# The layout of an intermediate in HBM: 512-byte pieces or 4-KB pieces

## The chip, the cores and the metric

One Trainium2 chip, all 8 cores. Each core computes one of the 8 batch elements with the same program, and the cores don't exchange data. The time is the device time of the slowest core in microseconds (us). The profile and the trace are of one execution, on the slowest core (core 4).

## The reference

```python
xn = layernorm(x)                                   # x: 8 x 2048 x 1024, f32
# attention, one head of width 1024, causal, softmax over all of (t, s)
q, k, v = xn @ Wq + bq, xn @ Wk + bk, xn @ Wv + bv
attn = softmax_all(mask(q @ k.T / 32)) @ v
# feed-forward on xn, int weights with scales per group of 128 rows
h  = layernorm(xn) * gamma + beta
y  = silu(h @ dequant(fc1_q, fc1_scales) + b1)      # 2048 x 4096 per core
z  = y @ dequant(fc2_q, fc2_scales) + b2            # 2048 x 1024 per core
out = x + attn + (xn + 0.5 * z)
```

Matrix products are done in bf16 with each operand split into a high and a low part; three of the four partial products are summed (`PAIRS`), so one product of a 128-row block over 1024 inputs is 24 matmuls (`mm24`).

## The kernel before

The stages follow each other: layernorm and q, k, v projections, attention, then fc1 and fc2. The engines run programs written out by hand and meet at semaphores.

fc1 goes over four blocks `tc` of 512 tokens and in each over 32 blocks `fc` of 128 hidden columns; one (`tc`, `fc`) is a unit `k` (`emit_fc1_unit`). A unit: TensorE does 24 matmuls of 512 columns into `P[k % 2]` (it waits for the Silu of unit k-2, which frees the bank); ScalarE applies Silu into `B_yf` (waits for TensorE and for GpSimd's unit k-2); GpSimd splits `B_yf` into a high and a low bf16 part in four buffers `B_yst[s2b][half]` (`s2b`: which 256 of the 512 tokens). Each buffer holds 8 units, 128 partitions by 8 x 256 bf16. After every eighth unit ScalarE's queue waits for GpSimd and then issues four stores of 512 KB, one for each buffer, into `hy` in HBM; GpSimd may begin the ninth unit only when all four have landed (`sy4`).

In `tc` 0 the fc1 weights are made at the same time (`emit_dq1_unit`, `emit_dq1_sub`): blocks of 8 dequantisation units, then 4 fc1 units. A dequantisation unit: VectorE forms (q - 128) * scale in PSUM from `B_dqq` and `B_dqs`, ScalarE copies it to bf16 `A_w1h` and then issues, from its own queue, the loads of `B_dqq` and `B_dqs` for the unit three further on; VectorE forms the low part `C_w1l`. So the ACT queue carries Silu, copies, weight loads and the stores of `hy` in one order.

fc2 reads `y` back in 8 groups of 256 tokens (`ygrp_load`), each in four quarters of 8 `fc`, high and low part: 64 loads of 512 KB from `hy` into `B_ygh` and `B_ygl`, issued on SP. The first group's `B_ygh` is loaded when `tc` 2 of fc1 has ended, its `B_ygl` when all of fc1's matmuls have. For the groups after it each quarter is loaded as soon as the matmuls of the group before have read it (`mmq`). Before the weights of fc2 are loaded into `B_dq2q` and `B_dq2s`, whose memory overlaps `B_yst`, SP waits for all stores of `hy` (L1285). The first group of fc2 runs beside the dequantisation of its weights, the other seven without it.

`hy` is `[4, 2, 2, NF, 128, 256]` in bf16: tc, s2b, half, fc, partition, token. In one store or load of 8 `fc`, a partition's 256 tokens of one `fc`, 512 B, are contiguous in HBM, and the next `fc` of that partition lies 64 KB further. In SBUF the same data are 4 KB in one piece per partition.

Of the kernel before, what the change touches and what calls it, by code (L numbers as in the profile page):

```python
# [8 lines left out]
BF16 = mybir.dt.bfloat16  # L9
# [10 lines left out]
NF = 32  # L20
# [16 lines left out]
def build_nc():  # L37
    nc = bass.Bass("TRN2", target_bir_lowering=False)
# [22 lines left out]
    hh = [nc.dram_tensor(f"hh{i}", [T, D], BF16, kind="Internal").ap() for i in range(2)]  # L61
    hqT = nc.dram_tensor("hqT", [NT, 2, 128, D], BF16, kind="Internal").ap()
    hattn = nc.dram_tensor("hattn", [NT, 128, D], F32, kind="Internal").ap()
    hy = nc.dram_tensor("hy", [4, 2, 2, NF, 128, 256], BF16, kind="Internal").ap()

    _rsv = nc.alloc_sbuf_tensor("arena_reserve", [128, 208704], mybir.dt.uint8)
    BASE = None
# [130 lines left out]
    def rd(eng, sem, out, in_, **kw):  # L198
        eng.dma_start(out=out, in_=in_, **kw).then_inc(sem.h, 16)  # L199
        sem.n += 16  # L200
        return sem.n

    def wr(eng, sem, out, in_):
        eng.dma_start(out=out, in_=in_).then_inc(sem.h, 16)  # L204
        sem.n += 16
        return sem.n

    with nc.Block() as block:
# [136 lines left out]
        def mm24(tensor, psum_ap, lhsT, rhsT, lslc, rslc):  # L345
            n = 0
            for g in range(ND):
                for (a, b) in PAIRS:
                    i = tensor.matmul(psum_ap, lhsT[a][lslc(g)], rhsT[b][rslc(g)],  # L349
                                      start=(n == 0), stop=(n == 23))  # L350
                    n += 1
            return i
# [771 lines left out]
        def emit_fc1_unit(tc, fc):  # L1124
            k = tc * NF + fc

            @block.tensor
            def _(tensor, tc=tc, fc=fc, k=k):
                if fc == 0:
                    tensor.wait_ge(lh[tc % 2].h, ht_ld[tc])  # L1130
                if tc == 0:
                    tensor.wait_ge(ve.h, ve_dqblk[fc // 4])
                if k >= 2:
                    tensor.wait_ge(ac.h, ac_y[k - 2])
                slot = tc % 2
                i = mm24(tensor, P[k % 2][:, 0:512], (A_w1h, C_w1l),
                         (B_hth[slot], B_htl[slot]),
                         lambda g, fc=fc: (slice(None), slice(g * FF + fc * 128, g * FF + (fc + 1) * 128)),
                         lambda g: (slice(None), slice(g * 512, (g + 1) * 512)))
                mm.inc(i)  # L1140
                mm_y[k] = mm.n

            @block.scalar
            def _(scalar, fc=fc, k=k):
                scalar.wait_ge(mm.h, mm_y[k])
                if k >= 2:
                    scalar.wait_ge(gp.h, ve_y[k - 2])
                i = scalar.activation(B_yf[k % 2][:], P[k % 2][:, 0:512], AF.Silu,  # L1148
                                      bias=M_b1T[:, fc:fc + 1])
                ac.inc(i)  # L1150
                ac_y[k] = ac.n

            @block.gpsimd
            def _(gpsimd, tc=tc, fc=fc, k=k):
                gpsimd.wait_ge(ac.h, ac_y[k])
                if k == 0:
                    gpsimd.wait_ge(sa[0].h, sa_t[NT - 1][0])
                    gpsimd.wait_ge(sa[1].h, sa_t[NT - 1][1])
                if fc % 8 == 0 and k >= 8:
                    tp, vp = sy_t[k - 1]  # L1160
                    gpsimd.wait_ge(sy4[tp].h, vp)
                c0 = (fc % 8) * 256
                gpsimd.tensor_copy(B_yst[0][0][:, c0:c0 + 256], B_yf[k % 2][:, 0:256])
                i = gpsimd.tensor_copy(B_yst[1][0][:, c0:c0 + 256], B_yf[k % 2][:, 256:512])  # L1164
                v_ = gp.inc(i)
                gpsimd.wait_ge(gp.h, v_)
                for s2b in range(2):
                    i = gpsimd.tensor_tensor(B_yst[s2b][1][:, c0:c0 + 256],  # L1168
                                             B_yf[k % 2][:, s2b * 256:(s2b + 1) * 256],
                                             B_yst[s2b][0][:, c0:c0 + 256], ALU.subtract)  # L1170
                gp.inc(i)
                ve_y[k] = gp.n

            if fc % 8 == 7:
                @block.scalar
                def _(scalar, tc=tc, fc=fc, k=k):
                    scalar.wait_ge(gp.h, ve_y[k])
                    fg = fc // 8
                    for s2b in range(2):
                        for half in range(2):  # L1180
                            wr(scalar, sy4[tc],
                               hy[tc, s2b, half, fg * 8:(fg + 1) * 8].rearrange("f p u -> p f u"),
                               B_yst[s2b][half].rearrange("p (f u) -> p f u", f=8))
                    sy_t[k] = (tc, sy4[tc].n)

# [53 lines left out]
        def ygrp_load(sync, grp, chase=False):  # L1239
            tc_, sub_ = grp // 2, grp % 2  # L1240
            sync.wait_ge(sy4[tc_].h, 256)
            for q4 in range(4):
                if chase:
                    if q4 < 3:
                        sync.wait_ge(mmq.h, (grp - 1) * 3 + q4 + 1)
                    else:
                        sync.wait_ge(mm.h, mm_z[grp - 1])
                for half in range(2):
                    dstb = (B_ygh, B_ygl)[half]
                    rd(sync, lyq[q4],  # L1250
                       dstb.rearrange("p (f u) -> p f u", f=NF)[:, q4 * 8:(q4 + 1) * 8, :],
                       hy[tc_, sub_, half, q4 * 8:(q4 + 1) * 8].rearrange("f p u -> p f u"))
                yq_ld[(grp, q4)] = lyq[q4].n

        @block.sync
        def _(sync):
            sync.wait_ge(mm.h, mm_tc_end[2])
            sync.wait_ge(sy4[0].h, 256)
            for q4 in range(4):
                rd(sync, lyq[q4],  # L1260
                   B_ygh.rearrange("p (f u) -> p f u", f=NF)[:, q4 * 8:(q4 + 1) * 8, :],
                   hy[0, 0, 0, q4 * 8:(q4 + 1) * 8].rearrange("f p u -> p f u"))

        @block.sync
        def _(sync):
            sync.wait_ge(mm.h, mm_tc_end[3])
            sync.wait_ge(sa[0].h, sa_t[NT - 1][0])
            sync.wait_ge(sa[1].h, sa_t[NT - 1][1])
            for q4 in range(4):
                rd(sync, lyq[q4],  # L1270
                   B_ygl.rearrange("p (f u) -> p f u", f=NF)[:, q4 * 8:(q4 + 1) * 8, :],
                   hy[0, 0, 1, q4 * 8:(q4 + 1) * 8].rearrange("f p u -> p f u"))
                yq_ld[(0, q4)] = lyq[q4].n


# [45 lines left out]
        for grp in range(8):  # L1321
            tc, sub = grp // 2, grp % 2

            @block.sync
            def _(sync, grp=grp, tc=tc, sub=sub):
                if grp >= 1:
                    ygrp_load(sync, grp, chase=True)
# [145 lines left out]
```

## Time and profile before

| | us |
|---|---|
| two runs | 2893.95, 3166.56 |
| their median | 3030.25 |
| the profiled execution | 2899.33 |
| its span, first to last instruction, core 4 | 2897.7 |
| spans of the 8 cores | 2875.2 to 2897.7 |
| TensorE busy | 2333.2 (81%) |
| ScalarE busy | 753.8 (26%) |
| VectorE busy | 681.9 (24%) |
| GpSimd busy | 274.7 (9%) |
| `hy` stores, ACT queue | 64 of 512 KB, 6.3 us to landing (median) |
| `B_ygh`, `B_ygl` loads, SP queue | 32 and 32 of 512 KB, 4.1 and 5.3 us |

The profiled execution stands beside the faster of the two runs, and everything read from the trace is compared with its own time. A busy share is an average over stages that have different limits, so the stages are read one by one.

### The profile page before, as it was taken

The page shows a single profiled execution, that of the slowest core. Times are in us where ns is not written, and L with a number is a line of the kernel's source. Part 1 is how long each engine was busy: PE and PEld are TensorE (multiplying, and loading weights), DVE is VectorE, ACT ScalarE, POOL GpSimd, SP SyncE. Part 2 cuts the span into 40 slices and gives each one's busy share as a digit, 9 for nine tenths or more (in the row PEclk, how much of TensorE's full clock was granted, in tenths as well). Part 3 has the DMA queues.
Part 4 walks back from the last instruction along what each step waited for, and adds up shares of the span by engine and source line. Part 5 has one row for each costly group of instructions (what it writes and reads, how often), then busy time and mean ns, then how long its engine had stood idle before and what let it go on. Part 6 is the DMA issues. An engine that isn't in the chain of part 4 may idle for free.

```text
span 2897.7 us, 26924 instructions; the slowest of 8 cores (2875.2 to 2897.7 us)
## 1 busy us (share of the span) xinstructions
PE 2333.2 (81%) x10500; PEld 1040.4 (36%) x10500; DVE 681.9 (24%) x910; ACT 753.8 (26%) x882; POOL 274.7 (9%) x547
## 2 busy tenths in 40 slices
PE   0349999997888887535659999999554899999998
PEld 0124444443333343212224444444211344444443
DVE  3422421113433324332220000000044311221122
ACT  3221321112222232146663333333244000000000
POOL 1000000000000000002213334334200000000000
PEclk9879999998778898757879999999855999999999
DMA  7524632213212110175442222231455422223330
GB/s 232 156 73 80 137 85 44 53 30 105 84 58 59 51 44 23 50 189 145 145 124 59 58 61 56 59 88 30 139 200 201 131 77 87 87 87 95 102 102 15
DMA packets 364558, 268.25 MB, mean 93 GB/s; under 512 B 181216, under 2 KB 312304, under 8 KB 364048
## 3 DMA queue, kind: packets, MB, share of 16 engines
q1 hardware_dynamic: 230016, 136.89, 17.3%
q10 hardware_dynamic: 131232, 107.50, 12.6%
q0 software_dynamic: 3184, 22.14, 2.3%
q8 instruction: 84, 1.38, 0.2%
q14 instruction: 42, 0.34, 0.0%
HBM read 157.41 MB, written 75.50 MB: 80 GB/s over the span
## 4 chain that ended last, share of the span: by engine, by line
PE 69%; ACT 9%; DMA 7%; DVE 6%; ACTq 4%; issue 3%; POOL 1%; SPq 1%; DVEq 0%; POOLq 0%
PE P L349 39%; PE P L1359 22%; PE P L860 8%; ACTq L204 3%; DMA B_dq2s<-s 2%; DMA B_dqs<-s 2%; DMA hxn<-B_sl 2%; ACT L1148 1%; ACT L1104 1%; SPq L199 1%; ACT L1307 1%; ACT B_yf L1148 1%; ACT L803 1%; DVE B_dq2f L1298 1%; DVE C_w2l L1315 1%
## 5 line engine op out<-in xcount | busy, mean ns | idle before, releaser
L349 PE MATMUL P<-B_hth,A_w1h 128*128 128x512 bf16 x1024 | 396.5, 387 | 152.8 <-ACT B_yf L1148 106.0
L1359 PE MATMUL P<-A_w2h,B_ygh 128*128 128x512 bf16 x1024 | 400.8, 391 | 113.7 <-DVE C_w2l L1315 113.7
L1359 PE MATMUL P<-A_w2h,B_ygl 128*128 128x512 bf16 x1024 | 402.8, 393 | 0.0
L1359 PE MATMUL P<-C_w2l,B_ygh 128*128 128x512 bf16 x1024 | 402.2, 393 | 0.0
L349 PE MATMUL P<-B_htl,A_w1h 128*128 128x512 bf16 x1024 | 396.2, 387 | 0.0
L349 PE MATMUL P<-B_hth,C_w1l 128*128 128x512 bf16 x1024 | 395.6, 386 | 0.0
L349 PE MATMUL P<-B_xth,C_wh 128*128 128x512 bf16 x512 | 196.4, 384 | 164.0 <-DMA B_xtl<-hxn 96.5
L1148 ACT ACT_TABLE_LOAD x128 | 164.2, 1283 | 398.5 <-PE P L349 306.3
L349 PEld LDWEIGHTS P<-B_hth,A_w1h 128*128 128x128 bf16 x1024 | 101.8, 99 | 285.3 <-issue 170.8
L349 PE MATMUL P<-B_xtl,C_wh 128*128 128x512 bf16 x512 | 196.2, 383 | 0.0
L349 PE MATMUL P<-B_xth,C_wl 128*128 128x512 bf16 x512 | 196.1, 383 | 0.0
L1359 PEld LDWEIGHTS P<-A_w2h,B_ygh 128*128 128x128 bf16 x1024 | 101.8, 99 | 261.8 <-issue 148.2
L1298 DVE SCALAR_TENSOR_TENSOR B_dq2f<-B_dq2q,B_dq2s 128x1024 f32<-128x1024 int32 x32 | 39.1, 1223 | 581.0 <-DMA B_dq2s<-s 580.6
L1168 POOL TENSOR_TENSOR B_yst<-B_yf,B_yst 128x256 bf16<-128x256 f32 x256 | 165.8, 669 | 19.3 <-POOL B_yst L1164 0.9
L1359 PEld LDWEIGHTS P<-A_w2h,B_ygl 128*128 128x128 bf16 x1024 | 103.0, 101 | 129.5 <-issue 15.2
L349 PEld LDWEIGHTS P<-B_hth,C_w1l 128*128 128x128 bf16 x1024 | 101.9, 100 | 126.2 <-issue 9.6
L349 PEld LDWEIGHTS P<-B_htl,A_w1h 128*128 128x128 bf16 x1024 | 101.7, 99 | 123.3 <-issue 8.2
L1359 PEld LDWEIGHTS P<-C_w2l,B_ygh 128*128 128x128 bf16 x1024 | 101.8, 99 | 121.7 <-issue 8.1
L1383 DVE TENSOR_SCALAR B_t<-B_xt,M_mu,M_r 128x512 f32<-128x512 f32 x32 | 17.4, 543 | 492.8 <-PE P L1359 484.3
L349 PEld LDWEIGHTS P<-B_xth,C_wh 128*128 128x128 bf16 x512 | 50.5, 99 | 226.6 <-issue 167.7
L776 ACT ACT_TABLE_LOAD x40 | 51.3, 1283 | 308.7 <-DVE B_ast L876 307.4
L860 PE MATMUL P<-C_vh,B_pth 128*128 128x512 bf16 x272 | 119.8, 441 | 13.0 <-DVE B_ptl L843 13.0
(147 smaller groups left out, 2599.3 us busy)
## 6 DMA issues: line engine op xcount, KB each, us to landing
hy<-B_yst ACTq DMA_DIRECT2D x64, 512.0 KB, 6.3
B_ygh<-hy SPq DMA_DIRECT2D x32, 512.0 KB, 4.1
B_ygl<-hy SPq DMA_DIRECT2D x32, 512.0 KB, 5.3
B_dq2q<-q SPq DMA_DIRECT2D x32, 512.0 KB, 3.9
B_dq2s<-s SPq DMA_DIRECT2D x32, 512.0 KB, 4.7
B_dqq<-q ACTq DMA_DIRECT2D x61, 256.0 KB, 3.8
B_dqs<-s ACTq DMA_DIRECT2D x61, 256.0 KB, 4.5
A_x<-x POOLq DMA_DIRECT2D x16, 512.0 KB, 27.6
```

Source lines behind the costliest of these rows:

```text
L199: eng.dma_start(out=out, in_=in_, **kw).then_inc(sem.h, 16)
L204: eng.dma_start(out=out, in_=in_).then_inc(sem.h, 16)
L349: i = tensor.matmul(psum_ap, lhsT[a][lslc(g)], rhsT[b][rslc(g)], start=(n == 0), stop=(n == 23))
L776: i = scalar.activation(B_pf[ch % 2][:, 0:w], B_sc[:, ch * 512:ch * 512 + w], AF.Exp, bias=M_negm[:, t:t + 1], accum_out=M_zc[:, ch:ch + 1])
L803: i = scalar.activation(B_sc[:, ch * 512:ch * 512 + w], P[ch % 2][:, 0:w], AF.Copy, scale=1.0 / 32.0)
L860: i = tensor.matmul(P[2 + h2][:, 0:512], (B_pth, B_ptl)[a][:, b * 128:(b + 1) * 128], (C_vh, C_vl)[c][:, b * D + h2 * 512:b * D + (h2 + 1) ...
L1104: i = scalar.activation(A_w1h[:, dst], PD1[k % 3][:, 0:512], AF.Copy)
L1148: i = scalar.activation(B_yf[k % 2][:], P[k % 2][:, 0:512], AF.Silu, bias=M_b1T[:, fc:fc + 1])
L1168: i = gpsimd.tensor_tensor(B_yst[s2b][1][:, c0:c0 + 256], B_yf[k % 2][:, s2b * 256:(s2b + 1) * 256], B_yst[s2b][0][:, c0:c0 + 256], ALU.su ...
L1298: i = vector.scalar_tensor_tensor(B_dq2f[fc % 2][:], B_dq2q[fc % 2][:], -128.0, B_dq2s[fc % 2][:], ALU.add, ALU.mult)
L1307: i = scalar.activation(A_w2h[:, dst], B_dq2f[fc % 2][:], AF.Copy)
L1359: i = tensor.matmul(P[pb + h2][:, 0:512], (B_ygh, B_ygl)[a][:, fc * 256 + jj * 128:fc * 256 + (jj + 1) * 128], (A_w2h, C_w2l)[c][:, fc * D ...
```

## The change

The dimension of partitions and that of `fc` change places in `hy`. Each partition's 32 x 256 values of one (tc, s2b, half) now lie in 16 KB in one row, and a store or load of 8 `fc` takes 4 KB of it per partition. Order, waits, queues and sizes of all transfers stay as they are.

```diff
-    hy = nc.dram_tensor("hy", [4, 2, 2, NF, 128, 256], BF16, kind="Internal").ap()
+    hy = nc.dram_tensor("hy", [4, 2, 2, 128, NF, 256], BF16, kind="Internal").ap()
...
                             wr(scalar, sy4[tc],
-                               hy[tc, s2b, half, fg * 8:(fg + 1) * 8].rearrange("f p u -> p f u"),
+                               hy[tc, s2b, half, :, fg * 8:(fg + 1) * 8],
                                B_yst[s2b][half].rearrange("p (f u) -> p f u", f=8))
...
                     rd(sync, lyq[q4],
                        dstb.rearrange("p (f u) -> p f u", f=NF)[:, q4 * 8:(q4 + 1) * 8, :],
-                       hy[tc_, sub_, half, q4 * 8:(q4 + 1) * 8].rearrange("f p u -> p f u"))
+                       hy[tc_, sub_, half, :, q4 * 8:(q4 + 1) * 8])
...
-                   hy[0, 0, 0, q4 * 8:(q4 + 1) * 8].rearrange("f p u -> p f u"))
+                   hy[0, 0, 0, :, q4 * 8:(q4 + 1) * 8])
...
-                   hy[0, 0, 1, q4 * 8:(q4 + 1) * 8].rearrange("f p u -> p f u"))
+                   hy[0, 0, 1, :, q4 * 8:(q4 + 1) * 8])
```

## Rows read from the trace of the kernel before

**Rows 1.** Page: granted TensorE clock in 40 slices, in tenths; DMA packets by size.
```profile
PEclk9879999998778898757879999999855999999999
DMA packets 364558, 268.25 MB, mean 93 GB/s; under 512 B 181216, under 2 KB 312304, under 8 KB 364048
```

**Rows 2.** Stages: us, busy (x) of PE, PEld, DVE, ACT, POOL; PEclk, DMA share, GB/s.
```profile
1243.00:1520.00 277.00, 151.45 (x624) 64.35 (x624) 84.06 (x128) 169.31 (x178) 48.48 (x96) 0.76 0.57 153
1520.00:2072.00 552.00, 534.95 (x2448) 239.65 (x2448) 0.00 (x0) 203.18 (x207) 210.80 (x416) 0.99 0.23 60
2259.00:2898.00 639.00, 625.13 (x2886) 282.77 (x2886) 127.63 (x193) 0.00 (x0) 0.00 (x0) 0.99 0.27 86
```

**Rows 3.** Chain of waits in fc1, tc 1 to 3: start us, us, what.
```profile
1566.66 31.25 PE P L349 x144
...
1857.24 0.37 ACTq L204
...
1859.68 1.48 ACTq L204
1861.30 1.28 ACT L1148
...
1863.43 31.25 PE P L349 x144
...
2035.64 31.25 PE P L349 x144
```

**Rows 4.** Waits, 1520 to 2072 us: who for whom, us, times, longest.
```profile
POOL B_yst L1163 <- DMA hy<-B_yst: 117.8, 12, 12.8
...
PE P L349 <- ACT B_yf L1148: 31.9, 13, 20.3
```

**Rows 5.** DMA issues: ns min/median/max; the page's landing, us; SP's timeline.
```profile
L204 ACTq DMA_DIRECT2D hy<-B_yst x64: 366/1336/4127, 1344.7 to 2077.6; - x64
...
L204 ACTq DMA_DIRECT2D hattn<-B_ast x16: 332/333/338, 688.1 to 1215.3; - x16
...
hattn<-B_ast ACTq DMA_DIRECT2D x16, 512.0 KB, 2.7
...
2396.20 0.34 SPq L199 DMA_DIRECT2D B_xt<-x  x1
...
2397.58 1.01 SPq L199 DMA_DIRECT2D B_at<-hattn  x1
```

**Rows 6.** Chain of waits in tc 0; last row: the page's median landing, us.
```profile
1344.75 0.39 ACTq L204
...
1351.94 5.45 DMA B_dqs<-s
...
1420.11 0.38 ACTq L204
...
1427.26 5.08 DMA B_dqs<-s
...
1494.21 0.38 ACTq L204
...
1501.68 6.06 DMA B_dqs<-s
...
B_dqs<-s ACTq DMA_DIRECT2D x61, 256.0 KB, 4.5
```

**Rows 7.** End of fc1: SP's loads in the timeline, then the chain of waits.
```profile
2067.07 3.94 SPq L199 DMA_DIRECT2D B_ygl<-hy  x4
...
2071.67 0.37 ACTq L204
...
2077.57 6.55 DMA hy<-B_yst
```

**Rows 8.** Stretches of 2 us, columns as in rows 2: the last two are DMA.
```profile
1649.00:1651.00 2.00, 1.86 (x9) 0.65 (x7) 0.00 (x0) 1.47 (x2) 0.00 (x0) 1.00 1.10 302
...
2317.00:2319.00 2.00, 2.00 (x11) 0.94 (x10) 0.00 (x0) 0.00 (x0) 0.00 (x0) 1.00 1.02 418
```

## The prediction

> **What bounds the kernel now.** I read the page's slices first, then the busy time by stage, then the chain of waits inside each stage, and last the issue and landing times of the DMAs that the change touches. The granted clock is the top digit wherever TensorE is busy, and the packet line says that most packets are small [rows 1]. By stage [rows 2]: in the first quarter of fc1 (`tc` 0, 277 us) TensorE works 151 us, so the dequantisation on ScalarE, VectorE and the ACT DMA queue sets the pace; in the rest of fc1 (552 us) TensorE is busy 535 us and is the bound but for small gaps; in the last 639 us, fc2 after its first group, it is busy 625 us and has nothing to gain. The small gaps of fc1 come once every 8 units (one unit is 24 matmuls for one `fc`): the chain leaves TensorE for the four stores of `hy` on ScalarE's queue, then a Silu, then TensorE again [rows 3]. TensorE waited for that Silu 13 times in this stage, 31.9 us, of which one wait of 20.3 us belongs to the dequantisation before it and 11.6 us to the 12 stores; GpSimd waited 12 times for the stores to land [rows 4].
>
> **What the change does to the transfers.** All of `hy` goes through 64 stores and 64 loads of 512 KB. `hy` now has pieces of 256 bf16, 512 B, so each transfer has 1024 pieces; 128 x 1024 = 131,072 packets, and the page counts 312304 - 181216 = 131,088 between 512 B and 2 KB [rows 1]. So practically all packets of that size are `hy`. After the change the 8 `fc` of one partition lie side by side: 128 pieces of 4 KB, 16,384 packets, at a pitch of 16 KB in HBM. Nothing else is added, removed or moved; no wait and no queue changes. The bytes are the same. What can change is (a) how long ScalarE's queue is held while it issues the four stores and (b) how fast 2.1 MB drain.
>
> (a) *Issue.* The first store of a group takes 0.37 us and the last 1.48 us even where the group is quick; the median of 64 is 1.34 us, the longest 4.13 us [rows 3, 5]. So it isn't the instruction that costs, it is the room behind it: the later ones are pushed back. The nearest rows with 4 KB pieces: the 16 writes of `hattn`, 0.33 us each, one at a time; and four 512 KB loads in a row on SP, the first 0.34 and the last 1.01 us, together 2.4 us from first start to last end [rows 5]. So four stores will cost 1.4 us (0.33 each with small gaps) to 2.4 us, against 3.9 us now at the least (1857.24 to 1861.16, [rows 3]). I take 2.4, since four in a row are what we have.
>
> (b) *Drain.* With `hy` stores alone in flight the core moves 302 GB/s; with 4 KB pieces in both directions (output writes beside loads of x and `hattn`) 418 GB/s [rows 8]. The DMA engines are fully busy in both, so the difference is the piece. I take 418 GB/s; the lower end is that the rate stays at about 300.
>
> The Trainium skill ("DMA: Bandwidth & Descriptors", section "Why small descriptors are slow (HBM only)") charges a fixed overhead of about 3 cycles on each packet beside one per 32 B, which is 19 for 16 at 512 B and 131 for 128 at 4 KB, a ratio of 1.16. By that estimate 302 would become 350 rather than 418 GB/s, and the drain terms below would be some 5 us smaller in sum, giving about 2871 us; no row here shows 350.
>
> **Term 1, the gaps of fc1, tc 1 to 3.** The run of TensorE between two gaps is 144 matmuls in 31.25 us; less the tail of the last (0.38 us), 30.87/143 x 24 = 5.18 us a unit. From the first of these starts to the last (1566.66 to 2035.64) there are 11 groups of 8 units: 468.98 us, where 88 x 5.18 = 455.9 [rows 3]. That is 13.1 us, 1.2 us each. The twelfth gap, before 1566.66, adds one more, and something of this recurs at unit borders anyway, since the waits themselves sum to 11.6 us for 12 [rows 4]: I take 13.5 us, bounds 11.6 and 15. Do they vanish? In a quick case the four issues run 1857.24 to 1861.16, then table load and Silu, and TensorE goes on at 1863.43. With 2.4 instead of 3.9 us the Silu is 1.5 us earlier, more than the mean gap; where the gap is larger the issue takes longer now, and it too falls to about 2.4. Two other units of TensorE run meanwhile and cover the rest. What is late next is GpSimd, which must not overwrite `B_yst` before the stores have landed: it waits 117.8/12 = 9.8 us from about the first issue [rows 4], so until 1867.0 in this case. The unit that starts at 1863.43 ends at 1868.6 and the one after it at 1873.8; by then its Silu (2.0 us) must be done, and before that GpSimd's 2.0 us for the ninth unit (210.80/104, [rows 2]): it may start at 1869.8. The slack is 2.8 us, and a faster drain only adds to it.
>
> **Term 2, the dequantisation in tc 0.** Here everything waits for ScalarE's queue. At three group borders (units 7, 15, 23) the chain is: first store issued, four issues, a copy to `A_w1h`, the issue of the next `B_dqq`/`B_dqs` load behind them, its landing. From first issue to landed `B_dqs`: 1344.75 to 1357.39, 1420.11 to 1432.34, 1494.21 to 1507.74, that is 12.6, 12.2 and 13.5 us [rows 6]. After: the same ring must still drain 2.1 MB of stores and 0.5 MB of the load in front of its end: 1.4 us until data move (`hattn` lands in 2.7 us [rows 5], of which 0.52 MB/418 GB/s = 1.25), plus 2.62/0.418 = 6.3, together 7.7 us. Saved 4.9 + 4.5 + 5.8 = 15 us. Lower bound, rate stays 300: 1.4 + 8.7 = 10.1, saved 8. Upper bound, the load lands as in the median after its issue, 4.5 us [rows 6], behind 1.4 us of stores and 0.8 of its own issues: 6.7, saved 18. ScalarE has three units already loaded to copy meanwhile and is not much ahead of the load even so, which is why I stay below that bound: 15.
>
> **Term 3, the end of fc1.** SP may load fc2's weights only once the last four stores have landed (their buffers overlap): 2071.67 to 2084.12, 12.45 us, all on the chain [rows 7]. SP sent the four `B_ygl` loads from 2067.07 on, so 4.19 MB drain together. At 418 GB/s from about 2068.5: 10.0 us, 2078.5, with the receipt 2079.5: saved 4.6 us. Lower bound: rate as now, 0. Upper: the stores do not feel the loads, 2.4 + 2.6 us = 5 us, saved 7.4.
>
> **Costed at nothing.** The fc2 loads of groups 1 to 7: each quarter is issued right after its last reader and needed most of a group later, and TensorE is busy 625 of 639 us [rows 2]; a group is 639/7 = 91 us, a quarter's last reader is in the second half and its next in the next group's first, half a group less an eighth later, 34 us, where a load needs about as long as a `B_dqs` load, 4.5 us [rows 6]. The store of unit 31 belongs to term 1.
>
> **The sum.** 13.5 + 15 + 4.6 = 33 us. It is made against the profiled execution's own 2899.3 us (span 2897.7 and 1.6 around it): **2866 us**. The median of the two runs shown, 3030, is halfway between 2894 and 3167; the profiled time stands beside the faster one, and the forecast belongs to that.
>
> **Rivals.**
> *Bytes decide, not pieces.* 4 KB writes drain no faster than now; only the issue shortens. For: no row has 4 KB writes alone; in [rows 8] they are mixed with loads. Against: the mix runs at 418 GB/s. Terms 13.5 + 8 + 0: 2878 us. Chance 0.16.
> *The change doesn't do what it says.* The pieces were merged or the issue is held by bytes, so nothing is gained: 2899 us. Against: the packet count fits 512 B exactly, and four 512 KB loads issue in 2.4 us. Chance 0.05.
> *The pitch hurts, slower than before.* 4 KB at every 16 KB from 128 partitions in step is an HBM pattern that no row shows; today's stores cover contiguous 64 KB blocks. If a group's drain (2.1 MB at 302 GB/s, 6.9 us) grows by x us, terms 2 and 3 cost 4x, and beyond GpSimd's slack of 2.8 us the 12 borders cost 12(x - 2.8), against 13.5 gained. It turns at x = 2.9 us, a drain of 9.8 us, 214 GB/s. At half the present rate, x = 6.9: 28 + 49 = 77 us, and with the issue pushed back again little of term 1 is gained: about 2976 us. Chance 0.04. The Trainium skill (same page, "Latency and other measured facts") lists losses for row pitches that are large powers of two, from 512 KiB up; 16 KiB is below its table, so its rule gives no loss here, and no run here has shown one.
> *More than the terms.* In tc 0 TensorE's granted clock is 0.76 of the higher level on the mean [rows 2], and it waits up to 20 us at a time; if shorter waits held the clock up, the 151 us of work there would take at best 624 x 0.216 us (30.87/143) = 135: 16 us more, 2850 us. Against: the wait shrinks from 20 to 15 us only. Chance 0.05.
>
> **How the numbers follow.** My forecast, 2866 us, has 0.70. Its terms' bounds give 2899.3 - 19.6 = 2880 and 2899.3 - 40 = 2859. The faster unprofiled run is 5 us below the profiled one, and the cores span 2875 to 2898, so the slowest of eight can fall a few us either way: range 2846 to 2888, which takes in the first rival and the last. About 2% (58 us), what a measurement of this kernel can tell from no change, is more than all terms at their upper bounds: faster by more 0.03, within 2% 0.92, slower 0.05 (the pitch, and what I haven't seen).
>
> **What would show each step.** Packets: about 115,000 fewer, almost none left between 512 B and 2 KB. Issue: median of `hy` stores near 0.4 us, four within 2.4. Term 1: TensorE's waits for the Silu in tc 1 to 3 near zero, groups of 8 units in 41.5 us. Term 2: first store issue to landed `B_dqs` 7 to 8 us. Term 3: last stores landed about 8 us after their first issue, not 12.4. The prediction is wrong if `hy` drains below 300 GB/s with 4 KB pieces, if the stall at the borders turns up as a GpSimd wait, or if the 15 us in tc 0 come back as waits for the next `B_dqs`.

## The result, and the profile after

| us | before | after |
|---|---|---|
| median (lowest to highest) | 2907.76 (2887.63 to 3287.06), 17 runs | 2877.21 (2868.15 to 3288.93), 18 runs |
| the profiled execution | 2899.33 | 2884.79 |
| spans of the 8 cores | 2875.2 to 2897.7 | 2861.7 to 2883.2 |

The ratio after to before is 0.9935, 95% interval 0.9908 to 0.9963: 18.9 us of 2899 (10.7 to 26.7), less than 2%, but a gain. (Some executions of any of these kernels are slowed as a whole by up to 15%; the medians in the table contain them, the ratios leave them out.) The forecast was 33 us less, 2866, range 2846 to 2888. The time lies in the range; the gain is little over half of what was summed, and 33 us lie outside its interval.

The page of after, TensorE's clock in 40 slices and the packets, answers [rows 1]:

```profile
PEclk9879999998888898758889999999755999999999
DMA packets 249870, 268.25 MB, mean 93 GB/s; under 512 B 181216, under 2 KB 181232, under 8 KB 249360
```

114,688 packets fewer, and 16 left between 512 B and 2 KB: the layout does what it says.

The two stages of fc1 on core 5, the slowest (columns as in [rows 2]):

```profile
1243.00:1520.00 277.00, 150.76 (x624) 64.15 (x624) 84.20 (x127) 166.94 (x175) 49.34 (x96) 0.76 0.60 154
1520.00:2055.00 535.00, 531.24 (x2448) 239.94 (x2448) 0.69 (x1) 203.74 (x208) 208.67 (x412) 0.99 0.19 60
```

The 2448 matmuls of the second stretch, which stood in 552 us, now stand in 535. The first stretch, where the forecast wanted 15 us, has the same 624 matmuls in the same 277 us. The border at 1520 us isn't quite that between `tc` 0 and `tc` 1, as the prediction has it: 2448 matmuls are 102 units, `tc` 1 to 3 and the last six units of `tc` 0.

One core of one execution is a poor scale for a few microseconds, so the further comparisons use all eight cores. The landmarks are the Silu of unit 0, of unit 31 and of unit 127 in the trace, and fc2's first and last dequantisation. Means over the cores, us:

| kernel | unit 0 to 31 (cores from-to) | 31 to 127 | 127 to fc2's first dequantisation | from there to its last |
|---|---|---|---|---|
| before | 261.2 (260.1-262.6) | 510.9 | 24.5 | 161.6 |
| after | 258.4 (253.6-262.1) | 497.5 | 22.9 | 160.9 |

So by stage the gain is 2.8 + 13.4 + 1.6 + 0.7 = 18.5 us, close to the measured 18.9. That the two agree so well is partly luck: in these two executions the cores of after came to unit 0 on the mean 4.6 us later (1287.9 against 1283.3 us), before `hy` is touched at all, and their whole spans differ by 14.2 us. The forecast's three terms were 15 (unit 0 to 31), 13.5 (31 to 127) and 4.6 us (127 to the first dequantisation).

The waits of core 5 from 1520 to 2062 us (who for whom, us, times, longest) answer [rows 4], and the chain there answers [rows 3]:

```profile
POOL B_yst L1163 <- DMA hy<-B_yst: 100.7, 12, 12.8
...
PE P L349 <- ACT B_yf L1148: 20.6, 2, 19.8
```

```profile
1561.19 0.33 ACTq L204
...
1563.14 10.63 DMA hy<-B_yst
...
1578.29 476.73 PE P L349 x2208
```

TensorE waited 13 times for a Silu before and waits twice now, and 19.8 of the 20.6 us is the wait for the dequantisation, which isn't this term's. The last row is the picture of term 1: 2208 matmuls, 92 units (24 matmuls each), without one gap in the chain, 476.73/92 = 5.18 us each. One stall is left, at unit 31, and it isn't a late Silu: the Silu stands behind GpSimd, and GpSimd behind stores that took 10.6 us to land from their last issue.

The four issues, from the list of DMA issues (ns, least/median/most), answer [rows 5]:

```profile
L204 ACTq DMA_DIRECT2D hy<-B_yst x64: 326/532/1288, 1347.0 to 2061.2; - x64
```

The median fell from 1336 to 532 ns and the longest from 4127 to 1288. In `tc` 0 the chain answers [rows 6]:

```profile
1346.99 0.33 ACTq L204
...
1348.66 1.26 ACTq L204
1351.23 7.55 DMA B_dqs<-s
...
1422.05 0.33 ACTq L204
...
1426.28 9.43 DMA B_dqs<-s
...
1497.27 0.33 ACTq L204
...
1501.51 8.12 DMA B_dqs<-s
```

From the first issue to the landed load: 11.8, 13.7 and 12.4 us, mean 12.6, where before had 12.6, 12.2 and 13.5. The issue is shorter (1346.99 to 1349.92, 2.9 us), but the landing behind it is later, 7.6 to 9.4 us in place of 5.1 to 6.1. Before, the stores were waited for at their issue; now they are waited for behind it.

The end of fc1 (chain, then SP's loads from the timeline) answers [rows 7]:

```profile
2059.80 0.33 ACTq L204
...
2061.18 11.00 DMA hy<-B_yst
```
```profile
2055.20 2.68 SPq L199 DMA_DIRECT2D B_ygl<-hy  x4
...
2072.25 0.33 SPq L199 DMA_DIRECT2D M_bvb<-bvb  x1
```

From first issue to landed on this core: 12.38 us, where before had 12.45.

### The profile page after: what moved, and what is told of

It reads as the page before. It is cut to its first block, busy times and chain, and to the rows that moved or that the text cites. A ratio compares the mean times of both kernels' runs of the same rounds, so it can differ in the third digit from the quotient of the medians.

```text
span 2883.2 us, 26924 instructions; the slowest of 8 cores (2861.7 to 2883.2 us)
## 1 busy us (share of the span) xinstructions
PE 2317.7 (80%) x10500; PEld 1037.3 (36%) x10500; DVE 682.5 (24%) x910; ACT 754.0 (26%) x882; POOL 275.5 (10%) x547
## 3 DMA queue, kind: packets, MB, share of 16 engines
q8 instruction: 84, 1.38, 0.2%
## 4 chain that ended last, share of the span: by engine, by line
PE 71%; DMA 8%; ACT 8%; DVE 6%; issue 3%; ACTq 2%; SPq 1%; POOL 1%; DVEq 0%; POOLq 0%
PE P L349 41%; PE P L1359 22%; PE P L860 7%; DMA B_dqs<-s 3%; DMA hxn<-B_sl 2%; DMA B_dq2s<-s 2%; ACTq L204 1%; ACT L1307 1%; DVE B_dq2f L1298 1%; DVE C_w2l L1315 1%; ACT L1104 1%; ACT A_w2h L1307 1%; ACT L803 1%; SPq L199 1%; PE PTp L836 1%
## 5 line engine op out<-in xcount | busy, mean ns | idle before, releaser
L860 PE MATMUL P<-C_vh,B_pth 128*128 128x512 bf16 x272 | 118.4, 435 | 12.9 <-DVE B_ptl L843 12.9
```

Of the source, the lines that this page charges most:

```text
L860: i = tensor.matmul(P[2 + h2][:, 0:512], (B_pth, B_ptl)[a][:, b * 128:(b + 1) * 128], (C_vh, C_vl)[c][:, b * D + h2 * 512:b * D + (h2 + 1) ...
```

## The experiments

All start from the kernel after, if not said otherwise. A time "0 to 31" is the mean over cores of the table's first stage, in one execution; after has 258.4. The experiments ran on three different chips of the same kind. A ratio is to runs of before on the same chip, the times by stage are not. "Border" is the place in `tc` 0 where the four stores of units 7, 15 and 23 are issued.

**Who is responsible for `tc` 0?** First, the weight loads on SP's queue instead of ScalarE's, so that they needn't stand behind the stores.

```diff
-                    rd(scalar, ldq[k % 3], B_dqq[k % 3][:], q1_h[g2, fb2])
...
+                @block.sync
...
+                    sync.wait_ge(ac.h, ac_cp1[k])
+                    rd(sync, ldq[k % 3], B_dqq[k % 3][:], q1_h[g2, fb2])
```

The transposed loads of `h` for `tc` 1, which SP issued in `tc` 0, move behind the weight loads here and in the next form.

> The kernel after, with the loads of B_dqq and B_dqs (units 3 to 63) issued by SP instead of ScalarE's queue; the transposes for tc 1 are issued after them on SP. Theory A (order in the ring): the weight load lands late at a group border of tc 0 because it stands behind 2.1 MB of stores in the same queue. Then from first store issued to landed B_dqs falls from 11.8 to 13.7 us to 6 to 9 us, the stretch from the first store of unit 7 to that of unit 31 (211.1 us in the mean of the cores) falls by 10 to 18 us, and the kernel takes about 2862 us. Theory B (the DMA engines carry no more here, whatever queue): landing stays above 10.5 us, the stretch stays within 4 us of 211, the kernel within 6 us of the one after.

Measured: ratio to before 1.0015 (0.9968 to 1.0063), 0 to 31 in 265.2 us, slower than after. SP issues a load once ScalarE's copy has ended, 2.0 us after VectorE has read the buffer (median); ScalarE's queue issued it 0.1 us after VectorE, ahead of the copy. That is paid by every unit, not only at three borders. So the edit changed the queue and the moment of issue at once, and can't tell the two apart. A second form let SP wait for VectorE instead (`sync.wait_ge(ve.h, ve_stt1[k])`):

> The first experiment again, with SP waiting for the VectorE step that reads B_dqq (as soon as the buffer is free) instead of for ScalarE's copy behind it. In the first one the load was issued about 2 us later than from ScalarE's queue, which hides what the separate queue is worth. If order in the ring is what delays the load at a border: the first waiting step runs 7 to 9 us after the first store issue, unit 0 to 31 takes 245 to 252 us. If not: 10 to 13 us and 256 or more.

0 to 31 in 247.2 us, 11 less than after and inside what was expected if the order in the queue is the cause (245 to 252). The other half of that expectation failed: at the borders the first dequantisation that waits for a load starts 11.9 us after the first store or later, not 7 to 9. But two units or more beyond after's one are through by then, because their loads were issued before the stores. The queue counts as well: from its own issue to its landing, the first `B_dqs` load that is issued after a border's first store takes 7.1 us in after, behind the stores (median of 24), and on SP's queue 3.9 us in the first form and 5.2 in the second. So both seem to help, and in the first form the later issue of every load outweighs it.

The stores of the three borders left out. GpSimd's waits for them go too, and fc2 reads unit 31's block four times in place of the missing ones, so part of `y` is wrong:

```diff
-            if fc % 8 == 7:
+            if fc % 8 == 7 and k in (7, 15, 23):
+                sy_t[k] = (tc, 0)
+            elif fc % 8 == 7:
```

> The kernel after, without the stores of units 7, 15 and 23 (12 of 64; the loads of tc 0 read the block of unit 31 four times, so part of y is wrong). It measures what these three borders cost in all: plain blocks of tc 0 take 32 to 33 us, blocks with a border 40 to 43 us. Theory A and B both expect the stretch from unit 7 to unit 31 to fall by 20 to 28 us from 211. If it falls by less than 12, most of what a border costs is not the stores at all but the Silu and the copies around them.

0 to 31 in 229.6 us (229.2 to 230.2). The stores of the borders cost 28.8 us, 9.6 each. That is their price with all that hangs on them, ScalarE's and GpSimd's waits included. So the place is right, there is more to be had than 15 us, and the cores agree within 1 us: the spread of after (253.6 to 262.1) comes with these stores.

The stores on SP's queue, the weight loads where they were. ScalarE then waits neither for GpSimd nor for the issue, and the first group's `B_ygh` loads, also on SP, are issued before `tc` 3's stores:

```diff
-                @block.scalar
+                @block.sync
                 def _(scalar, tc=tc, fc=fc, k=k):
```

> The kernel after, with all stores of hy issued by SP instead of ScalarE's queue (the B_ygh loads then stand behind unit 95's stores on SP, as in time before). ScalarE waits neither for GpSimd nor for the issue at a border: 2.4 + 2.9 us each at three borders of tc 0 leave the path, and the weight loads no longer stand behind the stores in one ring. If what is left of a border is mostly ScalarE being held and the order in the ring: unit 0 to 31 falls by 15 to 25 us from 258, the kernel takes about 2852 us. If it is the bytes that share engines and HBM: it falls by 0 to 8 us only, because the same 2.1 MB still delay the next weight load.

0 to 31 in 238.5 us (236.8 to 240.8), 20 less than after with the same bytes and pieces; 15 to 25 were expected. Its profiled execution took 2865.89 us (2852 expected); the runs are too few for a ratio.

**Is it the pitch?** 4 KB pieces that lie end to end instead of every 16 KB:

```diff
-    hy = nc.dram_tensor("hy", [4, 2, 2, 128, NF, 256], BF16, kind="Internal").ap()
+    hy = nc.dram_tensor("hy", [4, 2, 2, 4, 128, 2048], BF16, kind="Internal").ap()
...
```

> The kernel after, with hy as [4, 2, 2, 4, 128, 2048]: every store and load is one block of 512 KB, rows of 4 KB at a pitch of 4 KB instead of 16 KB. Theory C (the pitch of 16 KB slows the stores): an undisturbed group of stores lands in 6.0 us or less from its first issue instead of 7.0 us, the borders of tc 0 in 10 us or less instead of 12 to 13, the kernel is 8 to 12 us faster than the one after. If the pitch costs nothing: landing 7.0 us again, all stages within 1.5 us, the kernel the same within 0.2%.

Ratio to before 0.9963 (0.9922 to 1.0003), 0 to 31 in 253.4 us. The interval overlaps most of after's, so no gain is shown, and 5 us in one stage of one execution are inside the scatter that is shown further down. In `tc` 1 to 3 the four stores land 6.5 to 6.7 us after the first issue on all eight cores here, and on after's cores 0, 1, 6 and 7 as well. After's cores 2 to 5 need 6.9 to 8.4, but that isn't the pitch: the kernel `B_ygl` late further down has the same pitch of 16 KB and 6.5 to 6.7 us on all eight cores. What it is, the next experiment tells.

**Do the neighbours hold it up?** After, and then before, on one core alone; the other seven batch elements aren't computed.

```diff
-    res = run_bass_kernel_spmd(nc, in_maps, core_ids=list(range(8)))
+    res = run_bass_kernel_spmd(nc, in_maps[:1], core_ids=[0])
...
```

> The kernel after on one core alone (batch element 0; the other seven outputs are copies of it). Theory D (the two cores that share a stack of HBM get in each other's way once each asks for about 400 GB/s): alone, the first dequantisation that waits for a load at a border of tc 0 runs 8.5 to 9.5 us after the first store issue at all three borders (8 cores: 9.1 to 14.3, mean about 12), unit 0 to unit 31 takes 249 to 254 us (258.4), and the first load behind the last stores starts 9.5 us or less after their first issue (mean 10.9). If D is wrong, and the limit lies inside the core: 11 to 13 us at the borders, 257 to 260 us, 10.5 us or more.

> The kernel before on one core alone. Theory D: pieces of 512 B hold a core near 300 GB/s, so the neighbour hardly matters: borders 11.5 to 13 us as with 8 cores (mean 12.8), unit 0 to 31 258 to 262 us (261.2), last stores 11.5 to 12.5 us (12.3). Together with the other run, the change is then worth 25 to 32 us on a lone core where it is worth 19 on eight. If D is wrong, the two kernels differ by 15 to 20 us here too.

Spans 2836.0 and 2851.3 us: 15.3 between them, not the 25 or more that a hidden gain needs. 0 to 31: 248.9 and 254.1, 5.2 us between them; 31 to 127: 497.3 and 508.6. Both kernels lose in `tc` 0 when eight cores run, 9.5 us the one and 7.1 the other, so the expectation that the neighbour hardly matters at 512 B was wrong too. The second border, timeline of after alone and then of before alone (VectorE's row is the first dequantisation that waits):

```profile
1389.33 2.89 ACTq L204 DMA_DIRECT2D hy<-B_yst  x4
...
1398.19 0.70 DVE L1095 SCALAR_TENSOR_TENSOR P<-B_dqq,B_dqs 128x512 f32<-128x512 int32 x1 [0.68 <-DMA B_dqs<-s]
```
```profile
1388.83 3.95 ACTq L204 DMA_DIRECT2D hy<-B_yst  x4
...
1400.04 0.70 DVE L1095 SCALAR_TENSOR_TENSOR P<-B_dqq,B_dqs 128x512 f32<-128x512 int32 x1 [1.47 <-DMA B_dqs<-s]
```

8.9 and 11.2 us. Over the three borders: 10.1, 8.9, 8.7 against 12.1, 11.2, 11.2, so 2.3 us each, 6.8 in sum, is what the layout gives where nobody disturbs (the whole stage gained 5.2), and 15 us was never there. 2 us of pure stores, after alone and then before alone (the last column is GB/s):

```profile
1391.30:1393.30 2.00, 2.00 (x11) 0.89 (x10) 0.00 (x0) 1.00 (x1) 0.00 (x0) 1.00 1.02 406
```
```profile
1390.80:1392.80 2.00, 2.00 (x11) 0.89 (x10) 0.00 (x0) 0.00 (x0) 0.00 (x0) 1.00 0.98 275
```

The rates are near what the forecast took (418 and 302), and their ratio, 1.48, is even larger than its 1.38. It is the use of them that was wrong.

The eight-core traces show the neighbour at work. Cores are counted in pairs (0 and 1, 2 and 3, and so on), their times from each core's first instruction. In after, core 2 issues four stores at 1592.43 us and core 3 at 1595.29. Core 2, 2 us before and 2 us after core 3's stores start to move:

```profile
1594.40:1596.40 2.00, 2.00 (x11) 0.90 (x10) 0.00 (x0) 0.93 (x1) 0.00 (x0) 1.00 1.01 404
1596.40:1598.40 2.00, 2.00 (x11) 0.94 (x10) 0.00 (x0) 1.04 (x2) 0.00 (x0) 1.00 1.04 277
```

The landing of four stores in `tc` 1 and 2, where nothing else is in flight on the core, follows how far apart the two cores of a pair store (pieces of 4 KB; the last three rows are of the kernel stores on SP with `B_ygl` late, further down):

| pair | stores apart, us | first issue to last landing, us |
|---|---|---|
| after, cores 6 and 7 | 7.0 | 6.5, 6.5 |
| after, cores 0 and 1 | 3.8 | 6.5, 6.6 |
| after, cores 2 and 3 | 2.9 | 8.4, 8.2 |
| after, cores 4 and 5 | 2.0 | 7.4, 7.0 |
| stores on SP, late, cores 6 and 7 | 1.9 | 7.8, 7.2 |
| stores on SP, late, cores 0 and 1 | 0.3 | 9.2, 9.2 |
| stores on SP, late, cores 2 and 3 | 0.1 | 9.0, 9.0 |

**The size between.** Pieces of 1 KB:

```diff
+    hy = nc.dram_tensor("hy", [4, 2, 2, NF // 2, 128, 512], BF16, kind="Internal").ap()
...
```

> The kernel after with pieces of 1 KB (two fc side by side in hy). If a fixed cost for each piece explains 280 GB/s at 512 B and 400 at 4 KB (29.3 ns and 164 ns for one piece on one engine: 10 ns fixed and 0.0376 ns per byte), then 1 KB gives 48.5 ns, 338 GB/s: undisturbed stores land about 7.9 us after the first issue (9.0 and 6.7), and the four issues take 3.3 to 3.7 us. If it is a threshold instead, 1 KB equals one of its neighbours within 0.3 us.

Core 2, its four issues in the timeline and 2 us from 1.2 us after the first one:

```profile
1575.83 3.39 ACTq L204 DMA_DIRECT2D hy<-B_yst  x4
```
```profile
1577.00:1579.00 2.00, 2.00 (x11) 0.94 (x10) 0.00 (x0) 0.00 (x0) 0.00 (x0) 1.00 1.04 339
```

339 GB/s, as expected, and an undisturbed landing of 7.6 us from the first issue on cores 2 and 3, where 4 KB has 6.5 and 512 B 8.8. One of the 16 DMA engines' share gives an estimate of the time of a piece: 512 B/(280/16) = 29 ns, 1024/(339/16) = 48 ns, 4096/(402/16) = 163 ns. The line through them is 10 ns for every piece and 0.037 ns for every byte. The run took 2893.14 us, 0 to 31 in 257.1 us and 31 to 127 in 498.6: issues of 3.4 us close the gaps of TensorE almost as well as 2.9.

**The end of fc1.** The `B_ygl` loads behind the first loads of fc2's weights:

```diff
+            if fc == 1:
+                @block.sync
+                def _(sync):
+                    sync.wait_ge(mm.h, mm_tc_end[3])
...
+                        rd(sync, lyq[q4],
+                           B_ygl.rearrange("p (f u) -> p f u", f=NF)[:, q4 * 8:(q4 + 1) * 8, :],
+                           hy[0, 0, 1, :, q4 * 8:(q4 + 1) * 8])
```

> The kernel after, with the four loads of B_ygl for the first group of fc2 issued behind the first two pairs of fc2's weight loads instead of at the end of fc1's matmuls. If the last stores of hy are late because they share the engines with these 2.1 MB: landed 7 to 8 us after their first issue instead of 12.4, the first dequantisation of fc2 starts 4 to 5 us earlier after unit 127, and the kernel gains 3 to 5 us, of which the shifted loads may give back 1 to 2. If the stores themselves are slow there: landing stays above 10.5 us and nothing is gained.

Ratio to before 0.9923 (0.9872 to 0.9975). 127 to the first dequantisation in 20.3 us, 2.6 less than after (4 to 5 expected), of which 1.4 come back up to the last dequantisation. Core 5:

```profile
2035.54 2.92 ACTq L204 DMA_DIRECT2D hy<-B_yst  x4
2042.17 0.33 SPq L199 DMA_DIRECT2D M_bvb<-bvb  x1
...
2045.71 1.96 SPq L199 DMA_DIRECT2D B_ygl<-hy  x4
```

Without the loads beside them the last stores are landed (SP's next load is issued) 6.6 us after their first issue on one core of each pair; on the other it is 9.0 to 9.7 (cores 5 and 4: 6.6 and 9.7; cores 1 and 0: 6.7 and 9.0). The late one is in all four pairs the core that stores 4 to 8 us after its neighbour, when the neighbour's loads for fc2 have begun. In after, where the loads share the DMA engines, the eight cores have 9.3 to 13.0 us, mean 10.9, before 11.6 to 12.9, mean 12.4; in after, too, the later core of each pair lands later. So the small term has two causes: the core's own loads, and the neighbour's.

**Towards a better kernel.** Stores and loads all on SP, loads as early as in the second form above, `B_ygl` late:

```diff
+                    sync.wait_ge(ve.h, ve_stt1[k])
+                    rd(sync, ldq[k % 3], B_dqq[k % 3][:], q1_h[g2, fb2])
...
+                if g == 2 and held:
+                    held.pop()()
```

`held` keeps the four stores of a border until the next block's first three weight loads are issued.

> The kernel after with everything that the experiments so far point to: weight loads of tc 0 on SP as soon as the buffer is free, all stores of hy on SP (those of units 7, 15 and 23 behind the next block's first three weight loads), transposes for tc 1 at the end of tc 0, B_ygl behind the first two pairs of fc2's weight loads. Unit 0 to 31: without any stores it was 229.6 us, so 229 to 236 us. From unit 127 to the first dequantisation of fc2: 20 to 21.5 us. The kernel: 2842 to 2855 us, 1.4 to 1.9% faster than the kernel before. If stores that share the engines still delay the weight loads, 236 to 243 us and about 2858 us.

Ratio 0.9893 (0.9815 to 0.9972). 0 to 31 in 255.4 us; cores 0 to 5 have a granted clock of 0.89 to 0.90 there, and cores 6 and 7, with the usual 0.91, have 250.8 and 251.1 us. That is little or no gain in `tc` 0, where 229 to 236 were expected. SP and VectorE of core 7 in the timeline:

```profile
1330.97 3.27 SPq L204 DMA_DIRECT2D hy<-B_yst  x4
1334.34 1.23 SPq L199 DMA_DIRECT2D B_dqq<-q  x1
```
```profile
1345.88 0.70 DVE L1095 SCALAR_TENSOR_TENSOR P<-B_dqq,B_dqs 128x512 f32<-128x512 int32 x1 [8.85 <-DMA B_dqs<-s]
```

The fourth unit's loads and those after it stand behind the stores again, only on another engine's queue, and the first unit that waits for one of them comes 14.9 us after the first store (10.8 to 14.9 over all cores and borders). The same with the old 512 B pieces:

```diff
+    hy = nc.dram_tensor("hy", [4, 2, 2, NF, 128, 256], BF16, kind="Internal").ap()
```

> The kernel of the first run of this call with the old layout of hy, pieces of 512 B. It tells what the layout is worth once ScalarE isn't held by the stores and the weight loads don't stand behind them: unit 0 to 31 within 4 us of the 4 KB version, unit 31 to 127 (497.3) within 1 us since the issue no longer stands ahead of a Silu, the end of fc1 about 2 us longer; 3 to 7 us in all instead of 19. If the drain itself is what the layout buys, 10 us or more remain.

0 to 31 in 246.7 us, 31 to 127 in 497.3. The second number counts: with 512 B pieces, but the stores not on ScalarE's queue, `tc` 1 to 3 run as fast as after does. The first stands 9 us below its twin with 4 KB pieces (6 us on cores 6 and 7), where at most 4 us either way were expected. The pairs differ, though: at the first border its neighbours store 3 to 6 us apart, the twin's 0.3 to 2.6 us.

The stores on SP with 512 B pieces (the stores-on-SP kernel above, and `hy` as before):

> The sixth experiment (stores on SP, weight loads on ScalarE's queue) with the old layout, 512 B pieces. If the drain rate of the stores delays loads on another ring: first waiting step 2 to 3 us later than its 7.4 to 10.9, unit 0 to 31 244 to 248 us against 238.5. If packets of the two rings alternate, and a 512 B packet holds an engine shorter than the load's own 2 KB ones: equal or earlier, 236 to 240 us.

0 to 31 in 245.7 us, 31 to 127 in 498.4, and 31.3 to fc2's first dequantisation, 8 us more than after and 7 more than its 4 KB twin: here fc2's first weight loads stand behind the last stores and the `B_ygl` loads in SP's queue. 7 us in `tc` 0 (245.7 against 238.5) are within what was expected of the drain, but they can't be told from scatter, as the next kernel shows: stores on SP and `B_ygl` late, both edits as above.

> The kernel after with the stores of hy on SP (as in the sixth experiment, where unit 0 to 31 took 238.5 us) and B_ygl behind the first two pairs of fc2's weight loads (as in the third). Unit 0 to 31 again 237 to 241 us; from unit 127 to the first dequantisation of fc2 20 to 21.5 us instead of 24.6; 23 to 27 us faster than the kernel after in the stages from unit 0 on, the kernel about 2850 us, 1.3 to 2% faster than before.

Ratio 0.989 (0.9858 to 0.9923). Its code up to unit 31 is that of the kernel with 238.5 us, and it has 249.5, cores 0 to 3 at 253.5 and 4 to 7 at 243 to 247. The same code, 11 us apart, on two chips and in two executions. Beside the 512 B kernel just shown, which ran on the same chip, its 4 KB pieces even have 4 us more. What a single profile says of `tc` 0 to a few microseconds proves nothing, and this takes back the readings of 253.4 against 258.4 and of 255.4 against 246.7.

Much of this scatter goes with the neighbours. In the execution with 238.5 us the two cores of a pair issue their stores in `tc` 0 6 to 19 us apart; in the one with 249.5 us cores 0 to 3, at 253.5 us, store at most 1.3 us from their neighbours, and cores 4 to 7, at 243 to 247, 1.6 to 5.8 us. After and the kernel `B_ygl` late, which share their code up to unit 127, have 262 us for the pair that stores 0.9 us apart, 256 to 259 for those 1.9 to 5.1 us apart, 251 for those 5.5 and 7.2 us apart, and 248.9 on one core alone. That is a correlation; no run set the distance on purpose.

Last, on top of it, the first three loads of a block issued from ScalarE's queue before the block's last Silu, ahead of the stores:

```diff
+        def emit_dq1_early(fb):
+            @block.scalar
+            def _(scalar, fb=fb):
+                for k in range(fb * ND, fb * ND + 3):
+                    scalar.wait_ge(ve.h, ve_stt1[k])
...
+                    rd(scalar, ldq[k % 3], B_dqq[k % 3][:], q1_h[g2, fb2])
...
+                    if fc % 4 == 3 and fb + 1 < 8:
+                        emit_dq1_early(fb + 1)
```

> e11 and, in tc 0, the weight loads of each block's units 3 to 5 issued by ScalarE's queue ahead of the Silu of the last fc1 unit, as soon as their buffers are free, instead of behind the border. If the stall at a border is that these loads are issued after the stores, the first waiting step at 8 to 10 us after the first store goes (it runs at 6 to 7), and unit 0 to 31 takes 226 to 232 us, like or below the kernel without stores (229.6); the kernel about 2842 us. If the stores slow every load that runs beside them, whatever was issued first: 234 to 238.

Core 7 at the first border, ScalarE's queue, SP's, and VectorE:

```profile
1334.26 0.34 ACTq L199 DMA_DIRECT2D B_dqq<-q  x1
...
1336.54 0.45 ACTq L199 DMA_DIRECT2D B_dqs<-s  x1
```
```profile
1343.70 2.91 SPq L204 DMA_DIRECT2D hy<-B_yst  x4
```
```profile
1345.84 0.69 DVE L1095 SCALAR_TENSOR_TENSOR P<-B_dqq,B_dqs 128x512 f32<-128x512 int32 x1
1347.75 0.69 DVE L1095 SCALAR_TENSOR_TENSOR P<-B_dqq,B_dqs 128x512 f32<-128x512 int32 x1
1349.66 0.69 DVE L1095 SCALAR_TENSOR_TENSOR PSp<-B_dqq,B_dqs 128x512 f32<-128x512 int32 x1
```

The loads are out 7 us before the stores, and the three dequantisations that follow have no wait in their rows. 0 to 31 in 234.9 us, 5 above the 229.6 without any stores. That misses the 226 to 232 that were expected if the order of issue were all, and lies in the other range, 234 to 238: the stores still slow loads that run beside them. Ratio to before 0.987 (0.9838 to 0.9902), median 2859.33 us of 6 runs (2855.57 to 2867.87); the interval doesn't touch that of after. It is the fastest kernel here, but the runs of the kernel without the early loads (2860.67 to 2868.52, ratio 0.989) overlap with it, and its pairs stored 2.5 to 8.8 us apart, those of that kernel 0.3 to 5.8: how much of the 14.6 us in `tc` 0 is the early loads' isn't shown.

## Why the prediction was half right

**What bounds which stage** held: the gain lies where it was placed, and TensorE's granted clock did what it did before (0.76 and 0.99 of 2.4 GHz in both). The rival of a higher clock did not come.

**Term 1** was right in size and mechanism: 13.5 forecast, 13.4 us measured (11.3 on one core alone), groups without a gap, 5.18 us a unit, 114,688 packets fewer. Its input was off: the four issues take 2.9 us, median 532 ns, not 2.4 and 400, since stores are still pushed back. At a quick group of `tc` 1 to 3 four issues take 3.9 us before and 2.9 after, so the Silu is 1.0 us earlier, not 1.5. That is just enough: from one group's start to the next before had 42.4 us at the quick ones, where 8 x 5.18 = 41.4, and the mean of 1.2 us counts a few longer gaps (6.6 us of issue beside the `B_ygh` loads on core 4). That luck was in it, a saving of 1.0 us against a gap of 1.0, the prediction couldn't know. That it is ScalarE's queue being held and not the landing is shown by the two kernels with 512 B pieces and the stores on SP: 497.3 and 498.4 us. Those take GpSimd's wait off ScalarE's queue as well as the issue; after keeps that wait, so there it is the shorter issue.

**Term 2** is the step that failed: 15 us forecast, 2.8 measured on eight cores and 5.2 on one. It put 1.4 + 2.62/0.418 = 7.7 us for a border after, where 11.8, 13.7 and 12.4 us were measured, and subtracted it from *measured* borders of 12.2 to 13.5 us before. The same formula for before gives 1.4 + 2.62/0.302 = 10.1 us, 2.7 us short of what the trace showed. That remainder wasn't in the model, so it was credited to the change: 8 of the 15 us. Even the lower bound, "rate stays 300, saved 8", gave 8 us to a drain that had not changed at all. Where the remainder comes from is known only in part. One thing the model left out: the loads of three units, 1.57 MB, and not of one stand in the queue behind the stores when the first of them is waited for. But the first lands first, and the next dequantisation runs without a wait of its own. The timeline of after, core 5:

```profile
1422.05 2.93 ACTq L204 DMA_DIRECT2D hy<-B_yst  x4
...
1435.94 0.70 DVE L1095 SCALAR_TENSOR_TENSOR P<-B_dqq,B_dqs 128x512 f32<-128x512 int32 x1 [5.63 <-DMA B_dqs<-s]
1437.24 0.70 DVE L1095 SCALAR_TENSOR_TENSOR PSp<-B_dqq,B_dqs 128x512 f32<-128x512 int32 x1
```

The other is that, with eight cores running, the drain at these borders isn't the undisturbed one; the same border in a stretch of 2 us:

```profile
1428.00:1430.00 2.00, 0.00 (x0) 0.00 (x0) 0.73 (x2) 1.97 (x3) 0.00 (x0) 1.00 0.95 139
```

The DMA engines are 95% busy at 139 GB/s, with the neighbour's stores issued 1 us away. In the 12 us from the first store the cores of after move 218 to 317 GB/s, those of before 199 to 271.

The difference doesn't need the remainder. Only the stores have changed pieces, the loads have not, so the layout can save 2.1/0.28 - 2.1/0.402 = 2.3 us a border, 6.8 in all, whatever else is in the time, and that is what one core alone shows. The whole time is bracketed only: with one load behind the stores 1.4 + 2.1/0.28 + 0.52/0.418 = 10.1 us before and 7.9 after, with three 12.7 and 10.4, where 11.2 to 12.1 and 8.7 to 10.1 were measured. With 6.8 in place of 15 and the measured 1.6 for term 3 the sum is 13.5 + 6.8 + 1.6 = 22 us, 2877; that is worked out after the result, and three times the 2.3 us didn't show on eight cores.

**Term 3** was of the right kind and too large: 4.6 us forecast, 1.6 measured. It used the undisturbed 418 GB/s for 4.19 MB in both directions and so forecast 7.8 us to the landing; the cores measure 9.3 to 13.0 us, the later one of each pair late.

**Its inputs.** The 302 GB/s for 512 B is from a stretch whose DMA share reads 1.10 [rows 8]; stores of 512 B that nothing disturbs move 275 to 288. The signs that the prediction named as its own refutation came: the 15 us in `tc` 0 came back as waits for the next `B_dqs`, 11.8 to 13.7 us after the first store and not 7 to 8.

**Costed at nothing:** from fc2's last dequantisation to the end, its seven other groups (before 643.7 us, after 643.4) and GpSimd's landing wait in `tc` 1 to 3 stayed free, but for the one stall at unit 31, where the transposed loads of `h` still share the DMA engines.

**The rivals.** "Bytes decide, not pieces" gave 2878 us, next to the measured 2877, for a wrong reason: stores drain at 397 to 410 GB/s instead of 275 to 288. Its number fits because its 8 us for term 2 is the same error once more, and its 0 for term 3 happens to be near. "The pitch hurts" fell: 6.5 to 6.7 us of landing at 16 KB and at 4 KB alike. The Trainium skill ("DMA: Bandwidth & Descriptors", "Why small descriptors are slow (HBM only)") has a fixed overhead of about 3 cycles on each packet, and the trace agrees in kind; the size differs: the estimate from it gave a ratio of 1.16 between 512 B and 4 KB, where the runs show 402/280 = 1.44. The forecast preferred the rows, and there the rows were right.

**What stays open.** That the two cores of a pair slow each other's stores is shown in `tc` 1 and 2 (404 GB/s falls to 277); that this is also what makes the same code differ by 11 us in `tc` 0, and both kernels 7 to 9.5 us slower there on eight cores than on one, is argued from the distances, not shown. Which thing the pair shares, memory or another, no run here tells. With it stays open whether after really gains 2.8 us in `tc` 0 or the 5.2 of one core alone, since the two differ by less than that scatter, and how a border's time divides between the queue's order, the moment of issue and the sharing of the DMA engines.

## What to carry to other kernels

Let the model reproduce the measured time before you take its other case from it; what it can't explain of before belongs in both cases, and the gain is the difference of two models. A cheaper drain is worth something only where a queue waits for it, and there it is worth only the part of the queue's contents that got cheaper. Before making long transfers faster, issue the short loads ahead of them, and issue the stores from a queue in which nothing urgent stands: here that went with a `tc` 0 that is 9 to 24 us shorter, where the layout brought 2.8. Read a stage that is bound by transfers on all cores and in more than one execution, and look at when the neighbouring core does the same.

## What the runs showed of the hardware

- Stores alone in flight move 275 to 288 GB/s in pieces of 512 B (302 in [rows 8], where the DMA share reads 1.10), 339 at 1 KB, 397 to 410 at 4 KB. From 280, 339 and 402 GB/s, an estimate: a piece costs a DMA engine 10 ns beside 0.037 ns a byte.
- The issue of a DMA grows with the pieces of those just issued: four stores of 512 KB in a row take 3.9 us at 512 B, 3.4 at 1 KB, 2.9 at 4 KB, where a single one takes 0.33.
- Loads queued behind 2.1 MB of stores in one queue land late on whichever engine's queue it is: the first dequantisation that waits starts 9.1 to 14.3 us after the first store on ScalarE's queue, 10.8 to 14.9 on SP's. From issue to landing such a load takes 7.1 us on the median in after; on a queue that holds no stores it takes 3.9 and 5.2 (the two forms with the loads on SP).
- A 4-KB piece at a pitch of 16 KB lands like one at 4 KB: 6.5 to 6.7 us for four stores, both ways.
- Two neighbouring cores that store at the same time slow each other: 404 GB/s falls to 277 when the neighbour starts, and four stores of 4-KB pieces that land in 6.5 us at a distance of 3.8 us or more take 9.0 to 9.2 when the two are 0.1 to 0.3 us apart.
